# Early row tiles of a mixture-of-experts kernel: GpSimd's comparisons are split around two gathers' conditions, SyncE's stores and weight loads wait for landed tiles, and VectorE and TensorE reach the row table earlier

## The reference

```python
A_learned = sigmoid(sim) * (sim >= kth_largest(sim, 153))      # sim from ctx @ Wq, ctx @ Wk
A_learned = (A_learned + A_learned.T) * 0.5
x = x + tanh(g_xattn) * ((1 - gamma) * layernorm(x) + gamma * A_learned)

xt = layernorm(x).reshape(-1, 512)
probs = softmax(xt @ gate_w.T)                                 # 8 experts
weights, experts = top_k(probs, 2); weights /= weights.sum()
x1 = silu(xt @ w1[e].T); x3 = xt @ w3[e].T                     # 1024 columns each
x = x + tanh(g_ffn) * sum over the 2 experts of weight * ((x1 * x3) @ w2[e].T)
```

## Time and profile before

| | |
|---|---|
| median of 3 runs | 817.62 us (814.13 to 818.73) |
| the profiled execution, its own time | 819.66 us |
| its span, from the first to the last instruction | 818.0 us |
| TensorE busy | 731.9 us (89%) |
| VectorE busy | 414.4 us (51%) |
| ScalarE busy | 305.1 us (37%) |
| GpSimd busy | 169.8 us (21%) |
| mean granted TensorE clock | 0.938 of full speed |

### The profile page before, as it was taken

The page is one execution under the profiler, slowest core; times in us unless marked ns, Lnnn a source line. Parts: engine busy times, 40 slices in busy tenths (PEclk is TensorE's granted clock), DMA queues, the critical chain, the costliest instruction groups (busy, mean ns, idle before and its releaser), DMA issues.

```text
span 818.0 us, 10566 instructions
## 1 busy us (share of the span) xinstructions
PE 731.9 (89%) x3364; PEld 577.5 (71%) x3365; DVE 414.4 (51%) x1011; ACT 305.1 (37%) x497; POOL 169.8 (21%) x224
## 2 busy tenths in 40 slices
PE   7393089749899999999999999999999999999995
PEld 3193054537687888888888888888878888888884
DVE  3888977756265223823374247232832473374222
ACT  4844646611163113622272145221711452262121
POOL 2243001692111112111111211111112111111211
PEclk9755589898999999999999999999999999999998
DMA  8952053563136112741146127311551272111121
GB/s 297 378 234 103 0 206 106 219 221 116 40 114 246 26 26 39 260 112 26 26 128 231 30 41 286 80 26 26 149 210 37 38 292 70 26 26 26 28 42 34
DMA packets 23103, 94.52 MB, mean 116 GB/s; under 512 B 4336, under 2 KB 4592, under 8 KB 19248
## 3 DMA queue, kind: packets, MB, share of 16 engines
q1 hardware_dynamic: 14496, 70.54, 23.5%
q0 software_dynamic: 8448, 23.81, 14.2%
q10 hardware_dynamic: 144, 0.00, 0.0%
HBM read 74.02 MB, written 20.33 MB: 115 GB/s over the span
## 4 chain that ended last, share of the span: by engine, by line
issue 65%; POOL 9%; POOLq 3%; PE 2%; DMA 1%; DVE 0%; ACT 0%; DVEq 0%
POOL out L471 5%; POOL xtile L434 2%; POOL scratch L429 1%; DMA xtile<-found,rows_now 1%; POOLq L468 1%; POOLq L289 1%; PE bank L610 1%; PE bank L612 1%; PE bank L611 1%; POOLq L477 0%; PE bank L605 0%; ACT front L824 0%; DVE w_lo L1153 0%; PE bank L617 0%; POOLq L491 0%
## 5 line engine op out<-in xcount | busy, mean ns | idle before, releaser
L610 PE MATMUL bank<-w_hi,xT_hi 128*128 128x512 f32 x560 | 225.5, 403 | 1.2 <-DVE xT_lo L1333 1.2
L611 PE MATMUL bank<-w_hi,xT_lo 128*128 128x512 f32 x560 | 222.0, 396 | 0.0
L612 PE MATMUL bank<-w_lo,xT_hi 128*128 128x512 f32 x560 | 221.8, 396 | 0.0
L887 ACT ACTIVATE act_g<-bank 128x512 f32<-128x512 f32 x70 | 41.6, 595 | 283.7 <-PE bank L612 283.7
L610 PEld LDWEIGHTS bank<-w_hi,xT_hi 128*128 128x128 f32 x560 | 106.1, 189 | 25.3 <-issue 1.6
L612 PEld LDWEIGHTS bank<-w_lo,xT_hi 128*128 128x128 f32 x560 | 105.7, 189 | 25.6
L611 PEld LDWEIGHTS bank<-w_hi,xT_lo 128*128 128x128 f32 x560 | 106.1, 189 | 23.4
L610 PE MATMUL bank<-w_hi,hT_hi 128*128 128x512 f32 x280 | 116.5, 416 | 6.5 <-DVE hT_lo L1349 3.6
L1349 DVE TENSOR_TENSOR hT_lo<-bank,hT_hi 128x512 fp32r<-128x512 f32 x70 | 48.3, 691 | 129.6 <-ACT hT_hi L891 127.2
L1153 DVE TENSOR_TENSOR w_lo<-raw,w_hi 128x1024 fp32r<-128x1024 f32 x88 | 103.9, 1221 | 14.7 <-ACT w_hi L799 13.7
L612 PE MATMUL bank<-w_lo,hT_hi 128*128 128x512 f32 x280 | 110.1, 393 | 0.0
(11 more groups left out here) (227 smaller groups left out, 713.6 us busy)
## 6 DMA issues: line engine op xcount, KB each, us to landing
raw<-weights SPq DMA_DIRECT2D x24, 2048.0 KB, 7.7
xb<-x SPq DMA_DIRECT2D x4, 1024.0 KB, 12.4
raw<-xT SPq DMA_DIRECT2D x4, 1024.0 KB, 9.6
w_hi<-weights POOLq DMA_DIRECT2D x2, 2048.0 KB, 15.2
found<-xb SPq DMA_DIRECT2D x4, 1024.0 KB, 5.4
out<-xb SPq DMA_DIRECT2D x4, 1024.0 KB, 7.2
found<-scratch SPq DMA_DIRECT2D x1, 2092.0 KB, 29.8
front<-ctxT SPq DMA_DIRECT2D x4, 256.0 KB, 4.8
```

What stands on the lines that cost most here:

```text
L610: nc.tensor.matmul(out_ap, hi, hi_w, start=start, stop=False)
L611: nc.tensor.matmul(out_ap, lo, hi_w, start=False, stop=False)
L612: return nc.tensor.matmul(out_ap, hi, lo_w, start=False, stop=stop)
L887: nc.scalar.activation(act_g[:, s, :], bank[GATE[s]][:, :], ACT.Silu).then_inc(silu_set[s], 1)
```

## The change

On GpSimd the 16 comparisons of `columns_of(0)` are cut into groups of 3, 5 and 8, which stand ahead of `row_scales(2)`, ahead of `row_scales(3)` and behind it. SyncE waits for tile 1 in `xtile` ahead of the stores of batches 2 and 3, for tile 2 ahead of the loads of expert 1's weight groups 0 and 1, and for tile 3 ahead of group 2. TensorE does `all_blocks` in tile 2 some 12 matmuls earlier, ahead of the last parts of the first layer's s = 1. VectorE finishes the split of the last weight group before it takes tile 2's `x_low`, makes the row table's first part ahead of `h_low(0, 2)`, and puts six of its eight table copies behind tile 3's `x_low` and `scale_y`.

```diff
             store_meta(0)
+            sp.wait_ge(xtile_in, 16)
             store_x1(2)
             store_x1(3)
             store_meta(1)
...
-            next_weights(0)
+            sp.wait_ge(xtile_in, 32)
+            next_weights_of(0, 0)
+            next_weights_of(0, 1)
+            sp.wait_ge(xtile_in, 48)
+            next_weights_of(0, 2)
...
             gather(rows_now[:, 0:1])
+            columns_of(0, range(3))
             row_scales(2)
+            columns_of(0, range(3, 8))
             row_scales(3)
-            columns_of(0)
+            columns_of(0, range(8, PICKS))
...
+                if g == 1:
+                    all_blocks(0)
+                    all_blocks(1)
                 for c in range(2, DC):
                     if g == 0:
                         pe.wait_ge(lo_set[1], c + 1)
...
-                if g == 1:
-                    all_blocks(0)
-                    all_blocks(1)
                 pe.wait_ge(hT_set[0], nth)
...
             h_low(1, 1)
-            split_low(2, 0, [2])
+            split_low(2, 0, range(2, OPS))
             x_low(2, rows=False)
-            split_low(2, 0, [3])
             slots(0)
             scale_y(0, 0, OPS)
             take_meta()
             slots(1)
             tabulate()
             product(0, 2, 2 * OPS)
-            h_low(0, 2)
-            product(1, 2, 2 * OPS)
             order_blocks()
             place_columns([0])
             next_rows(2).then_inc(xtile_free, 1)
+            h_low(0, 2)
+            product(1, 2, 2 * OPS)
             h_low(1, 2)
-            place_columns(range(1, E))
+            place_columns([1])
             x_low(3)
             scale_y(0, 1, 2 * OPS)
             take_meta()
+            place_columns(range(2, E))
```

More of the change, by code:

```diff
@@ L345, in next_weights, with next_weights_of @@
                 for q in range(GROUPS):
-                    sp.wait_ge(lo_set[q], OPS * e + OPS)
-                    sp.dma_start(raw[:, q, :], w_groups[bass.ds(e + 1, 1), q, :, :].squeeze(0)).then_inc(raw_in[q], 16)
-            next_weights(0)
+                    next_weights_of(e, q)
+            def next_weights_of(e, q):
+                sp.wait_ge(lo_set[q], OPS * e + OPS)
+                sp.dma_start(raw[:, q, :], w_groups[bass.ds(e + 1, 1), q, :, :].squeeze(0)).then_inc(raw_in[q], 16)
+            sp.wait_ge(xtile_in, 32)
[3 more added lines that the diff above has]
+            next_weights_of(0, 2)
             with sp.Fori(1, E - 1) as e:
@@ L422, in row_scales, with columns_of @@
                 nc.gpsimd.tensor_tensor(meta[:, b, :, SHIFT - D], meta[:, b, :, SCALE - D], minus_mean[:, b, :], ALU.mult).then_inc(ln2_set, 1)
-            def columns_of(q):
+            def columns_of(q, picks):
                 pool.wait_ge(place_set, q + 1)
-                for m in range(PICKS):
+                for m in picks:
                     last = nc.gpsimd.tensor_scalar(in_column[q][:, m, :], columns[:, :], column[:, q, m // 2, m % 2:m % 2 + 1], 1.0,
                                                    ALU.is_equal, ALU.mult)
-                last.then_inc(column_set, 1)
+                if m == PICKS - 1:
+                    last.then_inc(column_set, 1)
             def gather(at):
@@ L484, in _ @@
             gather(rows_now[:, 0:1])
-            columns_of(1)
+            columns_of(1, range(PICKS))
             add_y(0, and_next_x=False)
```

## The result

The changed kernel takes **806.54 us** in the median of 4 runs (804.55 to 806.83), the kernel before 818.17 in the same comparison (4 runs, 814.13 to 819.28). The ratio is 0.9876, 95% interval 0.9841 to 0.9912. The profiled execution took 806.62 us, its span is 804.9 us. Against the profiled execution of before (819.66) it is 13.0 us shorter, against the median 11.6; 13.3 was forecast. Two runs of before on later chips, at 1083.75 and 1253.58 us with granted clocks of 0.64 and 0.56, belong to a slow state and are left out of every comparison.

What follows compares the result with a forecast made beforehand. TensorE, busy throughout the expert loops, was taken to lose time ahead of them, mostly to tile 2's late gather. 9.8 + 1.2 + 1.1 - 0.3 + 1.5 = 13.3 us off 817.6 gives 804.3 us, range 800.5 to 810.5.

Steps and rivals of the forecast that it cites:

- The 9.8 us of tile 2's wait: Ahead of tile 2's first layer: gather issued earlier and landing faster, wait hidden; 12.21 us becomes 2.41, 9.8 us gained.
- The clock in tile 2: Tile 2's first 42 large matmuls: TensorE's clock stays full, 11.10 us becomes 9.88, 1.2 us gained.
- the earlier table: Tile 2 to tile 3: earlier `all_blocks` lets tile 3's gather land in time; 13.53 us becomes 12.42, 1.1 us gained.
- Tile 1 (1.5, bounds 0 to 2.2): Tile 1's gather, with the stores held, lands at 146.7 instead of 149.1; 1.5 us gained, bounds 0 to 2.2.
- Rival (5): Tile 1's short wait keeps the clock up too, which saves 2 us: 802 us; chance 0.06.
- Six copies behind `scale_y`: In tile 3, VectorE's table copies use up the cover ahead of its product; 0.3 us lost, bounds 0 to 1.5.
- a sign of being wrong: Wrong if gather over 6 us, early slots wait for stores, or TensorE stands ahead of `all_blocks` or tile 3's h.
- The loops as long as before: Loops over experts, behind tile 3's start: left alone by the change, 605.56 us as before.
- Rival (2): Tile 2's gather is slow from GpSimd's and VectorE's work behind it, not from weights: 808.2 us; chance 0.25.
- Rival (3): The wait moves to VectorE, in tile 2 and ahead of the loop: gain 3 us, 814.5 us; chance 0.09.
- Rival (4): Slower: comparisons of 1.8 us each make TensorE stand at `all_blocks`, 824.3 us; decides from some 1.5 us each; chance 0.05.
- 0.90 beside a busy VectorE and 0.83 beside an idle one: GpSimd's time in us per comparison as read from the rows, held against Rival (4).

Runs made afterwards that it cites:

- e11: Kernel before with only the third weight load of each later expert held until the gather ahead of it has landed; 811.53 us, ratio 0.9965.
- e1: Changed kernel without SyncE's two waits ahead of expert 1's weight loads; 808.51 us, ratio 0.9923.
- e2: Kernel before with only SyncE's waits ahead of expert 1's weight loads added; 813.58 us, ratio 0.9986.
- e3: Changed kernel with GpSimd's first 16 comparisons in one piece again, behind both `row_scales`; 805.96 us, ratio 0.9911.
- e5: Changed kernel with `all_blocks` back behind tile 2's first layer and VectorE's second product ahead of the block numbers again; 808.05 us, ratio 0.9917.
- e4: Changed kernel without SyncE's wait for tile 1 ahead of the stores of batches 2 and 3; 806.48 us, ratio 0.9897.
- e7: Changed kernel with eight repeated comparisons added on GpSimd ahead of the block numbers; 809.54 us, ratio 0.9941.
- e8: Changed kernel with e6's moved copies and each later expert's third weight load held until the gather has landed, signalled by ScalarE; 809.69 us, ratio 0.9919.
- e6: Changed kernel with three of VectorE's six late table copies moved to its idle time ahead of `x_low(3)`; 806.12 us, ratio 0.9864.
- e9: Changed kernel with e6's moved copies and each later expert's third weight load held until the gather has landed, signalled by GpSimd; 800.85 us, ratio 0.9830.
- e10: e9 with the hold on each later expert's second weight load instead of the third; 801.21 us, one run.
- r1: Changed kernel run again, unedited; 806.35 us, ratio 0.9893.

## Why the prediction was right, and where it was not

The sum of 13.3 came out as 13.0 in the profiled pair, and the median (806.5) lies in the range. Step by step:

- **The 9.8 us of tile 2's wait**: 12.21 became 2.20 (2.41 forecast), 10.0. In e11, with the old order and loads, the same stretch is 10.97 (171.35 to 182.32), so some 1.2 us of the 12.21 was a late draw. The mechanism is shown by e1 (weights slow the gather), e2 (without VectorE's new order the wait goes to the split) and e3 (the comparisons' order is the small part).
- **The clock in tile 2 (1.2) and the earlier table (1.1)**: tile 2 to tile 3 took 22.63 us at full clock instead of 24.63 (187.81 to 212.44, granted clock 0.94), 2.0 for 2.3. The clock is the 1.2: the first 36 matmuls took 8.48 us (174.53 to 183.01), the pace of 42 in 9.9. That leaves 0.8 for the 1.1. `all_blocks` and the gather ahead of tile 3 are where they should be. That e5 loses 2.2 us does not contradict it: 2.00 of them are a wait for h that before did not have the earlier trace rows, because its slots began 2.7 us ahead of tile 2's first layer (185.13 and 187.81).
- **Tile 1 (1.5, bounds 0 to 2.2): the step that failed.** From the traced before to tile 2's transposes being wanted, 175.60 became 172.33, 3.3 us, over the upper bound (2.3 from the transposes' earlier start, 149.96 to 147.70, and 1.0 from the stretch behind it, 25.64 to 24.63 us). The held stores were not its cause: e4 does as well without. Nor was anything else in the change: e11, with the old order and free stores, starts tile 1's transposes at 146.19 and wants tile 2's at 171.35, both earlier than the changed kernel, and e2 is like it (146.26 and 171.12). What I had taken for the price of the stores was a late gather in one trace, so this term is worth nothing against runs of before such as these.
- **Rival (5), the clock in tile 1**: the granted clock there was 0.93 instead of 0.87, but TensorE's shorter wait is not shown to be the reason. With the same 1.65 us of wait as the changed kernel, e7 was granted 0.81 and took 26.5 us for this stretch, e8 was granted 1.00 and took 24.6, no less than the changed kernel at 0.93, for TensorE then waited longer for VectorE's early slots (1.01 us instead of 0.54).
- **Six copies behind `scale_y` (0.3 lost, bounds 0 to 1.5)**: 0.9, by e6; TensorE's 0.71 us ahead of tile 3's h is a wait that the prediction had named as a sign of being wrong.
- **"The loops as long as before"**: wrong by 2.2 us. 0.9 are the copies; the rest fits one late row more (three for two). The prediction had read only the loops' mean and had not seen those rows. The traces fit: over the 602.7 us of e9 and e10, and 0.9 more where the copies stand behind `scale_y`, the loops are 1.3 to 1.9 us longer for each late row, 1.5 in the mean over 22 rows in eight traces (e5's one row, of 0.23 us, and e8's others not counted); e7 and e11, without any, lie 0.5 us over and 0.6 us under that line.
- **Rival (2)**, the gather slow by what runs behind it, is refuted as the main cause by e2 and e3: with the loads held the gather took 4.7 and 4.3 us, with comparisons right behind it as before. A small part of it is true. The gather's own instruction took 1.9 to 2.0 us in before, e2, e3 and e11, where VectorE split weights beside it, and 1.2 in the changed kernel, where no split did; it lands 2.4 us behind the instruction's end in e3 and in the changed kernel alike. The Trainium skill's SBUF — State Buffer, section on the two separate sides, has a VectorE instruction with two SBUF inputs and a GpSimd instruction that reads SBUF shut each other out for a whole instruction; the comparisons agree, 2.81 us beside two splits for 0.73 (last section).
- **Rival (3)** is seen in small (0.45 and 0.71 us of TensorE for VectorE's h). **Rival (4)**'s comparisons took 0.92 us in the mean, far from 1.5; e7 adds 8.9 us and loses 2.0 to 2.5. The prediction's "0.90 beside a busy VectorE and 0.83 beside an idle one" mixes comparisons of two lengths (last section).

So 13.3 was right in part by luck: two errors of some 2 us, tile 1 and the loops, cancelled. Against the larger samples of before the change is worth less: 8 to 9 us by r1 (806.35 against 814.42, 0.9893), and 9.8 with the loops' late gathers out of both schedules (e9 and e11). Open is whether the change itself makes late gathers more frequent. Without the hold, the traces with tile 3 before 200 us have 1 to 4 of them, those with tile 3 after 200 none to 2, and I have no cause for that: in all ten traces without the hold, the second load is issued 4.1 us before the gather and the third 1.7 us behind it, to 0.1 us, whether it lands late or not.

## What to carry to other kernels

A transfer's time in one profiled execution can be a draw: before you build a term on a gather that took 6 us here and 3.5 there, look how often the same instruction does so elsewhere in the same trace, and list the few idle rows of a loop whose mean looks full. A small urgent gather should not share the DMA engines with bulk loads that nobody needs soon; let them wait for its landing, and take the signal from an engine that has nothing to do there. Where GpSimd is short of time, look at what kind of work VectorE does beside it and not at how busy it is. Moving a load is only half of it: read what the waiting engine does next (here a split of weights behind the same wait), or the time stays.

## What the runs showed of the hardware that I had not expected

- A load issued behind a gather can delay it. In the loops of the changed kernel the gather is issued at 237.47 for 1.33 us and the third load 0.4 us after that; the six such gathers landed after 4.1 to 8.0 us (in r1 4.5 to 8.0), at equal distances of issue. With that load held they took 4.1 to 4.65 (e9), with two held 3.7 to 3.83 (e10). The Trainium skill, DMA: Bandwidth & Descriptors, section on queues, rings and completion order, lets a completion wait for earlier writes; here the load that was issued later made the larger part of the delay.
- A comparison on GpSimd takes 0.73 us, and up to 2.81 us when VectorE splits weights (`w_lo<-raw,w_hi`, both inputs in SBUF) beside it. The 16 comparisons of the changed kernel, VectorE's splits beside them, then the real 16 of e7 (ns, min/median/max):

```profile
L437 POOL TENSOR_SCALAR xb<-columns,column x16: 731/768/2808, 167.2 to 181.2; 128x136 f16<-128x136 f16 x16
169.33 2.35 DVE L1164 TENSOR_TENSOR w_lo<-raw,w_hi 128x1024 fp32r<-128x1024 f32 x2
L437 POOL TENSOR_SCALAR xb<-columns,column x16: 736/751/869, 175.9 to 187.1; 128x136 f16<-128x136 f16 x16
```

VectorE was busy for 84% of the first 16 and for 92% of e7's, so it is not how busy it is that slows GpSimd: in e7 the splits had fallen beside the eight added comparisons, which took 8.55 us. The gather's instruction in the loops takes 1.33 to 1.38 us beside such a split and 1.06 to 1.08 elsewhere, which is the 0.3 us that e10's gathers still have over the others.
